# Four graph layers on one core: TensorE's signals in the edge stages move from the matmul to a drain behind it

## What is computed

```python
h = max(layernorm(x), 0)
x += concat(h, mean over edges of h[src]) @ W0.T + b0                      # layer 0
theta = h[dst] - h[src]                                                    # layer 1
x += segsum(sigmoid(relu(theta @ W1 + b1) @ W2 + b2) * theta) + indeg * (h @ W4 + b4)
h2 = relu(h @ Wp.T + bp)                                                   # layer 2
x += h + normalised(elu(mean(h2[src]) @ Wl.T + bl + h @ Wr.T))
x += segsum(norm * (h @ W_rel[type])[src]) + h @ W_loop                    # layer 3
```

## Time and profile before

| | |
|---|---|
| timed runs | 5464.44, 5466.43 (median), 5467.47 us |
| span of the profiled execution | 6426.8 us |
| PE busy, instructions | 3872.2 us (60%), 20122 |
| PE weight loads busy | 2959.4 us (46%) |
| DVE busy | 2933.5 us (46%) |
| ACT busy | 1413.8 us (22%) |
| POOL busy, instructions | 3972.3 us (62%), 4198 |
| granted TensorE clock, mean | 0.761 |

### The profile page before, as it was taken

The page is one execution under the profiler, slowest core; times in us unless marked ns, Lnnn a source line. Parts: engine busy times, 40 slices in busy tenths (PEclk is TensorE's granted clock), DMA queues, the critical chain, the costliest instruction groups (busy, mean ns, idle before and its releaser), DMA issues.

```text
span 6426.8 us, 68888 instructions
## 1 busy us (share of the span) xinstructions
PE 3872.2 (60%) x20122; PEld 2959.4 (46%) x20154; DVE 2933.5 (46%) x9989; ACT 1413.8 (22%) x5474; POOL 3972.3 (62%) x4198
## 2 busy tenths in 40 slices
PE   4676766655555565555555578876565565665433
PEld 3333434445544454455455456653344444444332
DVE  7555544556555565556555633342333222222222
ACT  4222122333333333333333401121000000000000
POOL 4556666456666666666666466646566666666665
PEclk7778778777777777777777789998777777777666
DMA  3333333345455454544545455555211111111121
GB/s 107 96 101 110 111 105 116 107 140 155 143 150 148 147 150 144 154 145 141 159 144 151 123 184 198 195 181 178 69 46 46 45 47 45 46 45 46 46 61 46
DMA packets 323521, 734.49 MB, mean 114 GB/s; under 512 B 77056, under 2 KB 164124, under 8 KB 310860
## 3 DMA queue, kind: packets, MB, share of 16 engines
q0 software_dynamic: 172432, 405.32, 23.2%
q1 hardware_dynamic: 148700, 323.81, 14.9%
q10 hardware_dynamic: 2016, 0.92, 0.1%
HBM read 598.71 MB, written 131.05 MB: 114 GB/s over the span
## 4 chain that ended last, share of the span: by engine, by line
another core or an unknown queue 30%; PE 27%; DVE 19%; issue 15%; ACT 4%; DMA 2%; DVEq 1%; SPq 1%; ACTq 0%
PE ps L2574 8%; DVE oneh L1863 6%; PE ps L2559 3%; PE ps L2530 3%; PE ps L2537 2%; DVE ps L1998 2%; PE ps L2469 2%; PE ps L2597 2%; DMA third<-dst_flat 2%; ACT turned_words L1681 1%; DVE third L1990 1%; PE ps L2419 1%; DVE turned_words L1955 1%; DVE tmp L1954 1%
## 5 line engine op out<-in xcount | busy, mean ns | idle before, releaser
L1470 POOL DMA_INDIRECT rows<-tab_rel,third x1299 | 1247.0, 960 | 646.9 <-issue 367.1
L1470 POOL DMA_INDIRECT rows<-tab_h,idx_src x1086 | 1046.7, 964 | 723.4 <-issue 345.8
L1470 POOL DMA_INDIRECT rows<-tab_hp,idx_src x1120 | 1077.1, 962 | 622.5 <-issue 298.8
L2597 PE MATMUL ps<-third 128*128 128x128 f32 x3126 | 607.1, 353 | 501.6 <-issue 295.8
L2530 PE MATMUL ps<-oneh,rows 128*128 128x128 f32 x2598 | 489.1, 340 | 607.1 <-DVE oneh L1863 330.7
L2597 PEld LDWEIGHTS ps<-third 128*128 128x128 f32 x3126 | 539.6, 258 | 593.7 <-issue 355.3
L2574 PE MATMUL ps<-third,h 128*120 128x384 bf16 (+17 forms) x3773 | 715.0, 337 | 65.8 <-issue 34.6
L2530 PEld LDWEIGHTS ps<-oneh,rows 128*128 128x128 f32 x2598 | 432.6, 245 | 695.8 <-DVE oneh L1863 362.6
L1681 ACT ACTIVATE turned_words<-turned_words 128x128 f32<-128x128 f32 x1563 | 463.1, 300 | 690.8 <-DVE turned_words L2003 527.5
L2574 PEld LDWEIGHTS ps<-third,h 128*120 128x120 bf16 (+10 forms) x3773 | 487.8, 133 | 239.4 <-issue 61.3
L1470 POOL DMA_INDIRECT third<-tab_hp,idx_src x443 | 425.9, 961 | 231.7 <-issue 118.5
(11 more groups left out here) (279 smaller groups left out, 5495.4 us busy)
## 6 DMA issues: line engine op xcount, KB each, us to landing
third<-dst_flat SPq DMA_DIRECT2D x390, 256.0 KB
h<-cnt_d SPq DMA_DIRECT2D x48, 1568.0 KB
cnt_d<-h SPq DMA_DIRECT2D x29, 1568.0 KB
cnt_d<-third SPq DMA_DIRECT2D x19, 1568.0 KB
tab_rel<-third SPq DMA_DIRECT2D x49, 512.0 KB
rows<-tab_rel,third POOLq DMA_INDIRECT x1299
rows<-tab_hp,idx_src POOLq DMA_INDIRECT x1120
rows<-tab_h,idx_src POOLq DMA_INDIRECT x1086
```

The source lines that it names most:

```text
L1470: pool.indirect_dma_start(out=to[:, t, 0:n], out_offset=None, in_=table[:, :], in_offset=bass.IndirectOffsetOnAxis(ap=idx[:, col:col + 1], ...
L2597: last = pe.matmul(ps_t[sl][:, t * P:(t + 1) * P], onehT[:, sl, t * P:(t + 1) * P], pwin[:, st["v"] % 2, :], start=True, stop=True)
```

## The change

Twelve `then_inc` of the edge stages in `tensor_program` move from the last matmul of a step to a `pe.drain()` behind it. Cut to its core:

```diff
@@ count3
-                    last.then_inc(s_count3.handle, 1)
+                    pe.drain().then_inc(s_count3.handle, 1)
@@ mult3, rels3
-                        last.then_inc(s_mult3.handle, 1)
+                        pe.drain().then_inc(s_mult3.handle, 1)
-                    last.then_inc(s_rels3.handle, 1)
+                    pe.drain().then_inc(s_rels3.handle, 1)
@@ put3
-                    pe.matmul(ps[4][:, 2 * P:2 * P + WIN], out3[0:n, :], place[0:n, st["u"] % 2, 0:WIN], start=True, stop=True
-                              ).then_inc(s_put3.handle, 1)
+                    pe.matmul(ps[4][:, 2 * P:2 * P + WIN], out3[0:n, :], place[0:n, st["u"] % 2, 0:WIN], start=True, stop=True)
+                    pe.drain().then_inc(s_put3.handle, 1)
@@ scatter_h and scatter
-                    last.then_inc(s_scat.handle, 1)
+                    pe.drain().then_inc(s_scat.handle, 1)
@@ rels_h, far_turn
-                    last.then_inc(s_hrel.handle, 1)
+                    pe.drain().then_inc(s_hrel.handle, 1)
-                    last.then_inc(s_gturn.handle, 1)
+                    pe.drain().then_inc(s_gturn.handle, 1)
@@ count (once for each bank that is read next)
-                            last.then_inc(s_count.handle, 1)
+                            pe.drain().then_inc(s_count.handle, 1)
@@ pack_mm, pack_turn, expand
-                        last.then_inc(s_pack.handle, 1)
+                        pe.drain().then_inc(s_pack.handle, 1)
-                    last.then_inc(s_turn.handle, 1)
+                    pe.drain().then_inc(s_turn.handle, 1)
-                    last.then_inc(s_expand.handle, 1)
+                    pe.drain().then_inc(s_expand.handle, 1)
```

## The result

The changed kernel takes 5740.5 us (5732.5 to 5752.9), the one before 5467.0 (5464.4 to 5467.8) on the same chips: a ratio of 1.0499, interval 1.0486 to 1.0512. It is 274 us slower, and outside the range.

The account below looks back on a forecast made before the run. It took POOL's gathers (1.25 us each, 5,080 of 6,427 us) plus late matmul signals as the bound. Sum: 5466 - 389 + 60 + 57 = 5,194, say 5,190 us; own range 4,790 (4,770 with margin) to 5,330, whole range 4,770 to 5,600.

Parts of the forecast that it names:

- What it takes away: POOL's remote waits in layers 1 and 3, 556 us, counted at 0.7: a gain of 389 us.
- The two clocks of this case: Span 960 us above the timed median, read as each of 4,064 gathers being 0.236 us cheaper when not profiled.
- a rival at 0.20: Lateness belongs to the profiled run: no waits to win, drains only cost, about 5,585 us; chance 0.20.
- The cost of a drain: On PE, where it has work ready: 0.26 us a drain in bf16, 0.36 in float32; nothing where PE waits.
- 196 more, of which I count 0.6: Layer 0 in the profiled-run rival (0.20): PE becomes the bound, stage takes 1,060 us; result 5466 + 118.
- The forecast's own term for layer 0: PE 948 against 946 us, two bounds of one size: 60 us of loss, between 0 and 119.
- Layer 2 was priced at 57: Layer 2: 496 + 57 = 553 us of PE against 496, a loss of 57 us (0 to 68).
- Completion itself is late: Rival: each drain holds PE's queue until the late acknowledgement; layer 1 at 2,546 us, kernel 6,040 or more; chance 0.08.

Follow-up runs that it names:

- the second profile: The kernel before, unchanged, profiled once more: 5466.1 us against 5466.5, with a span of 5465.3 us.
- the drain-behind run: Kernel before plus a drain behind each matmul that signals a count, signal left on the matmul: 5565.3 us (1.0185); on the slower chips 6566.7 (1.0317).

## Why the prediction was wrong

**The step that failed** is "What it takes away", 389 us. It took the remote waits for something that the timed kernel has. They were real in the execution that was profiled, but that execution is not one of the 5466 us kind: on such chips they are absent (no "remote" in any engine's waits of the second profile), and POOL has nothing to give back. Its premise, "if the drain's signal is not late", fails on the other kind of chip as well: 1,042 us of waits stay 1,046. Of the 546 us between 5,194 and the measured 5740, 389 are this term; the other 157 are the drains, priced at 60 + 57 = 117 and measured at 274.

**"The two clocks of this case"** was where it could have been seen. I took the 960 us between span and time for 0.236 us a gather. The second reading of the same number, gathers at 1.25 us and no remote waits, was written down as a rival at 0.20. It was right about the timed runs, by luck as to the reason: not the profiler's records, since with a span of 5465.3 the same profiler shows no such waits. The arithmetic that decides was there: 4,064 x 1.25 = 5,080 us and the stretches without gathers leave almost nothing of 5466. A guess of how much a profile costs should not have stood against that.

**The cost of a drain** was nearly right: 0.26 us forecast in bf16 and 0.36 in float32, 0.24 and 0.39 seen, though the two prices are not divided by type as forecast. The place was right too, layers 1 and 3 free, 0 and 2 not, and PE the bound of layer 0 over POOL's 864 us. The rival's "196 more, of which I count 0.6" is the term that was too small: layer 0 pays 205 in the profiled execution, the reduction by 0.6 had no row behind it. The forecast's own term for layer 0 was smaller still, 60 us, about the middle between 0 and 119. (That upper end is a slip: 730 + 330 - 946 is 114.) Layer 2 was priced at 57 and measured at 48, but the rival counted it at nothing, and the 29 us of node work behind both stages were in no term. 196 + 57 + 29 = 282 is the 274 measured, to 3%.

**"Completion itself is late"** (0.08) is what happens on the other kind of chip. I held against it that matmuls run on behind a late one; they do, but that shows nothing about when a drain lets go. Its price of +574 us is near the measured 6891 - 6370 = 521, but by luck: it put a drain in three at 2.8 us and all of it into layer 1. From the first profile to this run layer 0 grows by 251 us, layer 1 by 136, layer 2 by 46 (first gather to last).

**When a signal fires.** The Trainium skill, in "PSUM — Partial Sum Buffer", section "Engine vs sequencer instructions", says that an increment on a matmul fires on completion. The kernel before profiled again agrees: every wait for PE ends at a named matmul, none is "remote". On the other kind of chip the same rule holds if completion itself is late, as the drains say, and the section's sentence that a drain waits for the engine to go fully idle fits the 7.7 us for which `mult3` stood behind one. The Trainium skill, in "TensorE: Matmul & The Clock Gate", section "The cost: per-tile semaphore tail", adds some 26 ns for an increment; no run here measures that by itself, but it pointed to the right rival.

Nothing tried here beats the kernel before on either kind of chip. On the 5467 us kind POOL, at 1.25 us a gather, is 61% of the chain, and that is where an edit would have to start.

## To carry to other kernels

When a profile's span and the timed median differ by more than a per cent or two, profile the kernel again before costing anything, and test each stage against the bound of its steadiest engine: if count times period already fills the timed run, the waits in the trace are not in it. A drain on TensorE is worth a look only in a stage that another engine bounds, where it is free and gains nothing; in a stage that TensorE bounds it costs 0.24 to 0.39 us each, once TensorE's idle time is used up. If completion is late, a drain does not repair the signal, it moves the wait onto everything behind it.

## What the runs showed of the hardware

One kernel takes 5467 us on some chips and 6363 to 6370 on others, 16% more, steady within 0.5% on each. On the second kind matmuls complete microseconds late where POOL gathers; between the layers, without gathers, they do not the earlier trace rows. Only ACT, DVE and POOL have "remote" waits in the first profile and in the drain-behind run; PE, which waits for DVE and ACT, has none. The gathers take as long on both kinds (a median of 0.94 to 0.95 us). What in those chips does it was not found, and no run here separates the gathers from the rest of such a stage.

A drain that is issued behind a matmul which carries a signal itself ends later (47 ns against 21 ns behind the matmul). A second drain right behind the first adds 0.074 us in the trace and 0.1 us in the time of a bound stage.
